# Three pairs of banks for the gate and up products in the ternary feed-forward stages

## The chip, the cores and the metric

The kernel runs on one core of a Trainium2 chip. The metric is the device time of one execution in microseconds; lower is better. A core has five engines that run their own instruction streams and meet by semaphores: TensorE (PE in the rows; PEld are its weight loads), VectorE (DVE), ScalarE (ACT), GpSimd (POOL) and SyncE (SP), which issues DMAs. TensorE writes its products to PSUM, eight banks of 512 fp32 columns by 128 partitions, from which VectorE and ScalarE read them.

## The reference

Two layers on x, 2048 tokens of 256 numbers. Each is half a feed-forward part, attention, and half a feed-forward part again, each on the layer norm of x. The first layer's feed-forward part has ternary weights:

```python
gu = jnp.einsum('bsd,hd->bsh', x, wq_gu)
gate, up = jnp.split(gu, 2, axis=-1)
h = jax.nn.silu(gate) * up
hn = rms_norm(h)
return jnp.einsum('bsh,dh->bsd', hn, wq_p)      # x = x + 0.5 * this
```

h has 1024 columns. rms_norm divides each token's h by the root of its mean square plus eps. The second layer's feed-forward part has no such norm; it keeps the two largest of each four of h.

## The kernel before

It is a row of stages that follow each other with a barrier: set-up of the ternary weights, ffn0a (ternary, 63 to 185 us), attention with its projections, ffn0b (ternary, 723 to 847 us), then the same with the second layer's ffn1a and ffn1b. One function, `ffn_phase` (L299 on), writes all four feed-forward stages; `ternary` is true for the first two. Each engine's order is written out by hand in it.

A stage works through NB = 4 blocks of 512 tokens: block 0 alone, blocks 1 and 2 in a hardware loop, block 3 alone. A block has NCH = 8 chunks of 128 hidden columns. For chunk c of block b, with n = 8b + c:

- TensorE, `gate_up` (L361): 8 matmuls of 512 columns, 4 for gate and 4 for up (two halves of the input width, by high and low part of x). Gate goes to bank `slots[c]`, up to the next. In the ternary stages `slots` is 0, 2, 0, 2, ...: two pairs of banks. It first waits until the multiply of chunk n-2 is done (the semaphore `mul` at n-1).
- ScalarE, `silu` (L431), from the gate bank into one of two buffers. Behind it, for the chunk before: `hi` (L438), the high part of h, and the square (L447). Both wait for the multiply of their chunk, so silu of chunk c+1 is queued behind the multiply of chunk c-1.
- VectorE, `multiply` (L485): h = silu x up bank. Behind it `lo` (L490), the low part of h of the chunk before.
- GpSimd adds the squares of a block up (L590, L593) and takes powers: the inverse of a deviation for layer norm (L136) and of the root mean square (L597).

Between the chunks stand, in TensorE's order: behind chunk 2 `squares` of block b-1 (L383, sums of squares over partitions, into 4 columns of bank 4) and the second half of `down` of block b-1 (L372, 32 matmuls); behind chunk 6 the eight `transposes` of block b+1's normalised x (L143, into banks TB and TB+1, here 4 and 5); behind chunk 7 the first half of `down` of block b, 32 matmuls into banks 6 and 7, which first waits for `residual` of block b-1. In VectorE's order: behind chunk 1 the statistics of block b+1; behind chunk 3 `mean_squares` of block b-1 (L524, reads the 4 columns), then the normalisation of block b+1 (L124, four instructions); behind chunk 6 `residual` of block b-1 (L532, four instructions, reads banks 6 and 7); before chunk 7's multiply the low part of the transposed x (L158), after ScalarE's high part (L151).

In the text "multiply 4" is the multiply of chunk 4 of the block spoken of, and so on.

Of the kernel before, what the change touches and what calls it, by code (L numbers as in the profile page):

```python
# [24 lines left out]
ALU = mybir.AluOpType  # L25
# [3 lines left out]
P = 128  # L29
# [4 lines left out]
NB = TOK // BLK  # L34
TPB = BLK // P
# [3 lines left out]
HID = 4 * D  # L39
NCH = HID // P  # L40
# [13 lines left out]
RMS_EPS = float(np.finfo(np.float32).eps)  # L54
# [7 lines left out]
def named(g, nc, prefix, names):  # L62

    sems = [nc.alloc_semaphore(name=f"{prefix}_{n}") for n in names.split()]
    g.sems += sems
    return namedtuple("Semaphores", names)(*sems)
# [14 lines left out]
def blocks_of(eng, body):  # L81

    body(0)
    with eng.Fori(1, NB - 1) as b:
        body(b)
    body(NB - 1)


def is_first(b):
    return isinstance(b, int) and b == 0  # L90


def is_last(b):
    return isinstance(b, int) and b == NB - 1
# [44 lines left out]
def pe_transpose(e, g, s, b, src, bank=0):  # L139

    for k in range(KD):
        for j in range(TPB):
            ins = e.transpose(g.ps[:, bank + k, j * P:(j + 1) * P], src(j, k), g.ident[:, :])  # L143
    ins.then_inc(s.tr, 1)
# [9 lines left out]
def dve_lo(e, g, s, b, bank=0, half=None):  # L154
    xh, xl = (g.xh, g.xl) if half is None else (g.xh[:, half], g.xl[:, half])
    for k in range(KD):
        e.wait_ge(s.xhi, b * KD + k + 1)
        e.tensor_tensor(xl[:, k, :], g.ps[:, bank + k, :], xh[:, k, :].bitcast(F32), ALU.subtract).then_inc(s.xlo, 1)  # L158
# [140 lines left out]
def ffn_phase(nc, g, name, ternary, out=None, ahead=()):  # L299
# [12 lines left out]
    with ExitStack() as ctx:  # L312
        s = named(g, nc, name, names)

        def sb(n, shape, dt):
            return ctx.enter_context(nc.sbuf_tensor(f"{name}_{n}", shape, dt))
# [6 lines left out]
        if ternary:  # L323
            sq = sb("sq", [P, 2, BLK], F32)
            ssq = sb("ssq", [P, 2, BLK], F32)
            ms, inv = sb("ms", [P, TPB], F32), sb("inv", [P, TPB], F32)
            w_up = [g.wt[:, 0:KD * 2 * HID].rearrange("p (k h) -> p k h", k=KD)]
            w_dn = [g.wt[:, KD * 2 * HID:].rearrange("p (c d) -> p c d", c=NCH)]
            terms = [(0, 0), (0, 1)]
            hs = h32  # L330
            slots, TB = (0, 2, 0, 2, 0, 2, 0, 2), 4
        else:
            ab = sb("abs", [P, 2, GCH, BLK], F32)
            win = sb("win", [P, 6, BLK], BF16)
            rank = sb("rank", [P, GCH, BLK], BF16)
            w_up = [t[:, :].rearrange("p (k h) -> p k h", k=KD) for t in (g.wgu_h, g.wgu_l)]
            w_dn = [t[:, :].rearrange("p (c d) -> p c d", c=NCH) for t in (g.wdn_h, g.wdn_l)]
            terms = [(0, 0), (0, 1), (1, 0)]
            hs = ab
            slots, TB = (0, 2, 4, 0, 2, 4, 0, 4), 2  # L340
        xp, hp = [g.xh, g.xl], [hh, hl]
        block = ctx.enter_context(nc.Block())

# [1 line left out]
        @block.tensor  # L345
        def _(e):
            def gate_up(b, c):
                n = b * NCH + c

                if ternary:  # L350
                    if not (is_first(b) and c < 2):
                        e.wait_ge(s.mul, n - 1)
                elif not (is_first(b) and c < 3) and c != 1:
                    e.wait_ge(s.mul, n - 1 if c in (0, NCH - 1) else n - 2)
                for half in range(2):
                    col = half * HID + c * P
                    for k in range(KD):
                        if c == 0 and half == 0:
                            e.wait_ge(s.xlo, b * KD + k + 1)
                        for q, (w, x) in enumerate(terms):  # L360
                            ins = e.matmul(g.ps[:, slots[c] + half, :], w_up[w][:, k, col:col + P], xp[x][:, k, :],  # L361
                                           start=k == 0 and q == 0, stop=k == KD - 1 and q == len(terms) - 1)
                ins.then_inc(s.gu, 1)

            def down(b, u, tiles=range(TPB)):
                e.wait_ge(s.hlo, b * NCH + u * GCH + GCH)
                if u == 0 and not is_first(b):
                    e.wait_ge(s.res, b)
                for j in tiles:
                    todo = [(i, w, x) for i in range(GCH) for w, x in terms]  # L370
                    for q, (i, w, x) in enumerate(todo):
                        ins = e.matmul(g.ps[:, 6 + j // 2, (j % 2) * D:(j % 2 + 1) * D], hp[x][:, u, i, j * P:(j + 1) * P],  # L372
                                       w_dn[w][:, u * GCH + i, :], start=u == 0 and q == 0 and j % 2 == 0,
                                       stop=u == 1 and q == len(todo) - 1, skip_group_check=True)
                if j == TPB - 1:
                    ins.then_inc(s.dn if u else s.dnh, 1)

            def squares(b):

                e.wait_ge(s.sqc, b * NCH + NCH)  # L380
                for j in range(TPB):
                    for u in range(2):
                        ins = e.matmul(g.ps[:, 4, j:j + 1], ssq[:, u, j * P:(j + 1) * P], g.one_col[:, :],  # L383
                                       start=j == 0 and u == 0, stop=u == 1, skip_group_check=True)
                ins.then_inc(s.sqs, 1)

            def transposes(b):
                e.wait_ge(s.xn, b + 1)
                if not is_first(b):
                    if ternary and not (isinstance(b, int) and b == 1):  # L390
                        e.wait_ge(s.ms, b - 1)
                    if not ternary:
                        e.wait_ge(s.mul, b * NCH - 3)
                pe_transpose(e, g, s, b, lambda j, k: g.xn[:, j, k * P:(k + 1) * P], TB)

            def body(b):
                for c in range(NCH):
                    gate_up(b, c)
                    if ternary:
                        if c == 2 and not is_first(b):  # L400
                            squares(b - 1)
                            down(b - 1, 1)
                        if c == NCH - 1:
                            down(b, 0)
                    elif not is_first(b):
                        if c == 4:
                            down(b - 1, 0)
                        if c == NCH - 2 and not is_last(b):
                            down(b - 1, 1, range(TPB // 2))
                        if c == NCH - 1:  # L410
                            down(b - 1, 1, range(0 if is_last(b) else TPB // 2, TPB))
                    if c == NCH - 2 and not is_last(b):
                        transposes(b + 1)

            transposes(0)
            blocks_of(e, body)
            if ternary:
                squares(NB - 1)
            else:
                down(NB - 1, 0)  # L420
            down(NB - 1, 1)
# [57 lines left out]
        def _(e):  # L479
# [41 lines left out]

            def mean_squares(b):
                e.wait_ge(s.sqs, b + 1)
                e.tensor_scalar(ms[:, :], g.ps[:, 4, 0:TPB], 4.0 / HID, 4.0 * RMS_EPS, ALU.mult, ALU.add).then_inc(s.ms, 1)  # L524

            def residual(b):
                if ternary:
# [8 lines left out]
            def body(b):  # L536
                for c in range(NCH):
                    if c == NCH - 1 and not is_last(b):
                        dve_lo(e, g, s, b + 1, TB)
                    multiply(b, c)  # L540
                    if ternary:
                        if c:
                            lo(b, c - 1)
                        elif not is_first(b):
                            lo(b - 1, NCH - 1)
                        if c == 3 and not is_first(b):
                            mean_squares(b - 1)
                        if c == 6 and not is_first(b):
                            residual(b - 1)
                    elif c >= GCH:  # L550
                        choose(b, 0, c - GCH)
                    elif not is_first(b):
                        choose(b - 1, 1, c)
                    if not is_last(b) and c == 1:
                        dve_stats(e, g, s, b + 1)
                    if not is_last(b) and c == (3 if ternary else 5):
                        dve_normalise(e, g, s, b + 1)
                if not ternary and not is_first(b) and not is_last(b):
                    residual(b - 1)
# [1021 lines left out]
```

## Time and profile before

| | us |
|---|---|
| median of 3 runs | 1806.38 |
| lowest, highest run | 1805.32, 1822.72 |
| the profiled execution: its time | 1802.62 |
| the profiled execution: its span | 1800.4 |

In the rows, a timeline line gives start, duration, engine, line, operation, output<-input, and in brackets how long the engine had been idle and what released it. Recorded ends of matmuls overlap the start of the next one, so the distance between two starts is what one costs.

### The profile page before, as it was taken

Reading aid. Unit: us, or ns where it says so; the run is one execution under the profiler, and the core shown is the slowest. Engines: PE = TensorE matmul, PEld = TensorE weight load, DVE = VectorE, ACT = ScalarE, POOL = GpSimd, SP = SyncE. Lnnn points to the kernel's source line nnn. Section 1 sums busy time; section 2 is a strip of 40 time slices with the busy share of each in tenths; the row PEclk is TensorE's granted clock in tenths of the full one; section 3 lists DMA queues with packets and bytes.
Section 4 is the critical chain, followed back from the end, with each engine's and each line's share of the span. In section 5 each row is a group of like instructions: output and inputs, shape, how many; then the busy total and the mean of one; then the engine's idle time right before and its main releaser. Section 6 shows DMA issues by size and latency. Waiting matters only on the chain. (4 is left out here: it accounts for less than half of the span.)

```text
span 1800.4 us, 33059 instructions
## 1 busy us (share of the span) xinstructions
PE 1556.4 (86%) x13324; PEld 972.3 (54%) x13324; DVE 1283.4 (71%) x1864; ACT 950.9 (53%) x1889; POOL 306.7 (17%) x326
## 2 busy tenths in 40 slices
PE   1598878989999999887799689899999999997996
PEld 0487744444434436676588567444444444366885
DVE  8655647888898832564599786687888988025996
ACT  3345324767777784454334222456686788733342
POOL 5333100000000000232043432000000000030433
PEclk9999869999999999898899888698999999788998
DMA  5000769100000000100100058640000000020000
GB/s 201 24 1 0 127 184 129 34 14 24 13 20 7 2 2 3 46 1 24 35 1 1 1 116 199 87 69 14 20 17 16 11 2 2 2 71 1 12 12 24
DMA packets 37857, 70.54 MB, mean 39 GB/s; under 512 B 5411, under 2 KB 13219, under 8 KB 36645
## 3 DMA queue, kind: packets, MB, share of 16 engines
q1 hardware_dynamic: 37716, 68.58, 16.8%
q8 instruction: 99, 1.62, 0.4%
q14 instruction: 42, 0.34, 0.1%
HBM read 48.90 MB, written 22.15 MB: 39 GB/s over the span
## 5 line engine op out<-in xcount | busy, mean ns | idle before, releaser
L1166 DVE TENSOR_REDUCE l_att_maxima<-psum 128x2 f32<-128x1024 f32 (+3 forms) x640 | 665.0, 1063 | 135.3 <-PE psum L1064 127.6
L1258 ACT ACTIVATE l_att_probs<-psum 128x512 f32<-128x512 f32 (+3 forms) x1280 | 605.6, 531 | 250.3 <-PE psum L1092 227.8
L1109 PE MATMUL psum<-l_att_probs,l_att_v 128*17 128x256 f32 (+2 forms) x4608 | 363.5, 389 | 1.2 <-ACT l_att_o L1265 0.9
L1092 PE MATMUL psum<-l_att_qt,l_kt 51*128 51x512 f32 (+6 forms) x1280 | 331.6, 470 | 7.5 <-ACT l_att_probs L1258 7.5
L1064 PE MATMUL psum<-l_kt,l_att_qt 59*128 59x512 f32 (+7 forms) x1280 | 285.2, 422 | 5.0 <-DVE l_att_maxima L1166 2.6
L1092 PEld LDWEIGHTS psum<-l_att_qt,l_kt 59*128 59x128 f32 (+1 forms) x1280 | 142.6, 194 | 174.0 <-ACT l_att_probs L1258 161.8
L1109 PEld LDWEIGHTS psum<-l_att_probs,l_att_v 128*17 128x17 f32 x4608 | 79.5, 96 | 150.5 <-issue 101.7
L1064 PEld LDWEIGHTS psum<-l_kt,l_att_qt 59*128 59x128 f32 (+1 forms) x1280 | 139.1, 199 | 19.5 <-DVE l_att_maxima L1166 17.4
L1228 POOL CAST l_att_crow<-l_att_cneg 128x16 bf16<-128x16 f32 x32 | 8.1, 252 | 812.6 <-DVE l_att_cneg L1176 812.6
L1061 PE MATMUL psum<-tri 64*128 64x128 bf16 x1024 | 89.1, 237 | 22.0 <-DVE l_att_maxima L1166 18.8
L1090 PEld LDWEIGHTS psum<-tri 64*128 64x128 bf16 x1024 | 33.7, 96 | 101.8 <-ACT l_att_probs L1258 65.6
L1090 PE MATMUL psum<-tri 64*128 64x128 bf16 x1024 | 82.4, 228 | 1.9 <-DMA l_att_qt<-l_att_ct 1.7
L1193 DVE RECIPROCAL l_att_rinv<-psum 128x16 f32<-128x16 f32 x32 | 8.0, 250 | 106.3 <-PE psum L1128 106.3
L1061 PEld LDWEIGHTS psum<-tri 64*128 64x128 bf16 x1024 | 35.8, 101 | 59.8 <-DVE l_att_maxima L1166 34.3
L580 POOL TENSOR_TENSOR ffn1b_hl<-ffn1b_abs,ffn1b_hh 128x512 fp32r<-128x512 f32 x32 | 51.7, 1643 | 84.6 <-ACT ffn1b_hh L438 84.6
L580 POOL TENSOR_TENSOR ffn1a_hl<-ffn1a_abs,ffn1a_hh 128x512 fp32r<-128x512 f32 x32 | 51.7, 1644 | 84.6 <-ACT ffn1a_hh L438 84.6
L136 POOL TENSOR_TENSOR rstd<-var,mhalf 128x4 f32<-128x4 f32 x24 | 24.7, 1027 | 224.8 <-DVE var L115 224.8
L361 PE MATMUL psum<-ffn0b_xh,w_ternary 128*128 128x512 f32 x128 | 53.1, 415 | 9.2 <-DVE ffn0b_h L485 7.8
L361 PE MATMUL psum<-ffn0a_xh,w_ternary 128*128 128x512 f32 x128 | 52.9, 413 | 9.1 <-DVE ffn0a_h L485 7.7
L361 PE MATMUL psum<-ffn1b_xh,wgu_h 128*128 128x512 f32 x128 | 51.5, 402 | 3.9 <-DVE ffn1b_xl L158 2.8
L361 PE MATMUL psum<-ffn1a_xh,wgu_h 128*128 128x512 f32 x128 | 51.3, 400 | 3.9 <-DVE ffn1a_xl L158 2.8
L372 PE MATMUL psum<-wdn_h,ffn1b_hh 128*128 128x256 f32 x128 | 38.8, 303 | 15.6 <-DVE x_resident L532 8.9
(205 smaller groups left out, 2914.5 us busy)
## 6 DMA issues: line engine op xcount, KB each, us to landing
l_kt<-qk_scratch SPq DMA_DIRECT2D x48, 256.0 KB, 10.6
qk_scratch<-l_att_kv_parts SPq DMA_DIRECT2D x22, 512.0 KB, 7.3
l_att_qt<-qk_scratch SPq DMA_DIRECT2D x168, 64.0 KB
qk_scratch<-y SPq DMA_DIRECT2D x10, 512.0 KB, 10.7
set_raw<-in_w_gu SPq DMA_DIRECT2D x2, 1024.0 KB, 6.4
x_resident<-in_x SPq DMA_DIRECT2D x1, 2048.0 KB, 15.4
y<-in_w_gu SPq DMA_DIRECT2D x1, 2048.0 KB, 8.1
raw_down<-in_w_dn SPq DMA_DIRECT2D x2, 1024.0 KB, 8.0
```

The lines of the kernel that those rows point to most:

```text
L136: e.tensor_tensor(g.rstd[:, :], g.var[:, :], g.mhalf[:, :], ALU.pow).then_inc(s.rstd, 1)
L361: ins = e.matmul(g.ps[:, slots[c] + half, :], w_up[w][:, k, col:col + P], xp[x][:, k, :], start=k == 0 and q == 0, stop=k == KD - 1 and q ...
L372: ins = e.matmul(g.ps[:, 6 + j // 2, (j % 2) * D:(j % 2 + 1) * D], hp[x][:, u, i, j * P:(j + 1) * P], w_dn[w][:, u * GCH + i, :], start=u ...
L580: e.tensor_tensor(hl[:, c // GCH, c % GCH, :], hs[:, c // GCH, c % GCH, :], hh[:, c // GCH, c % GCH, :].bitcast(F32), ALU.subtract).then_i ...
L1061: e.matmul(g.ps[:, bank + x, w - P:w], g.tri[half, (2 + m) * P:(3 + m) * P], g.tri[half, m * P:(m + 1) * P], start=m == 0, stop=False, ski ...
L1064: e.matmul(g.ps[:, bank + x, 0:w], qt[rows_of(x), pair, t * P:(t + 1) * P], g.kt[rows_of(x), pair, c * BLK:c * BLK + w], start=c < qb, sto ...
L1090: e.matmul(g.ps[:, i % SB, off:off + P], g.tri[rows, c * P:(c + 1) * P], g.tri[rows, (2 + c) * P:(3 + c) * P], start=c == 0, stop=False, s ...
L1092: e.matmul(g.ps[:, i % SB, off:BLK], g.kt[rows_of(x), hp, kt * P:(kt + 1) * P], qt[rows_of(x), hp, off:BLK], start=u >= TPB, stop=True, sk ...
L1109: ins = e.matmul(g.ps[h * VW:h * VW + HD + 1, OB, lo:hi], g.v[:, kt, STEPS[st][1] * HG + h, :], pr[:, un % PB, h, lo:hi], start=u == 0 and ...
L1166: e.tensor_reduce(mp[:, st % 2, 2 * p:2 * p + 2, t, c], g.ps[:, bank:bank + 2, 0:w], AX.X, ALU.max).then_inc(s.mx, 1)
L1228: e.tensor_copy(cr[:, 0], whole).then_inc(s.cp, 1)
L1258: e.activation(pr[:, un % PB, h, off:BLK], g.ps[:, i % SB, off:BLK], ACT.Exp, scale=HD ** -0.5).then_inc(s.ex, 1)
```

## The change

In the ternary stages too, gate and up now go through three pairs of banks in the order 0, 2, 4, 0, 2, 4, 0, 4, and the transposes through banks 2 and 3 (TB = 2). `gate_up` waits for the multiply that read its pair last: of chunk n-3, for chunks 0 and 7 of chunk n-2; chunk 1 waits for none. The transposes wait for multiply 4 of the block in which they stand, in place of `mean_squares`. `squares` goes to bank TB and waits for multiply 1 of its block, the last reader of that bank. `mean_squares` moves on VectorE from behind chunk 3 to behind chunk 2, and chunk 4, the next to write that bank, waits for it. The stages of the second layer keep their order.

```diff
-            slots, TB = (0, 2, 0, 2, 0, 2, 0, 2), 4
         else:
...
-            slots, TB = (0, 2, 4, 0, 2, 4, 0, 4), 2
+        slots, TB = (0, 2, 4, 0, 2, 4, 0, 4), 2
...
-                if ternary:
-                    if not (is_first(b) and c < 2):
-                        e.wait_ge(s.mul, n - 1)
-                elif not (is_first(b) and c < 3) and c != 1:
+                if not (is_first(b) and c < 3) and c != 1:
                     e.wait_ge(s.mul, n - 1 if c in (0, NCH - 1) else n - 2)
+                if ternary and c == 4 and not is_first(b):
+                    e.wait_ge(s.ms, b)
...
-            def squares(b):
+            def squares(b, last):
 
                 e.wait_ge(s.sqc, b * NCH + NCH)
+                e.wait_ge(s.mul, last)
                 for j in range(TPB):
                     for u in range(2):
-                        ins = e.matmul(g.ps[:, 4, j:j + 1], ssq[:, u, j * P:(j + 1) * P], g.one_col[:, :],
+                        ins = e.matmul(g.ps[:, TB, j:j + 1], ssq[:, u, j * P:(j + 1) * P], g.one_col[:, :],
...
                 if not is_first(b):
-                    if ternary and not (isinstance(b, int) and b == 1):
-                        e.wait_ge(s.ms, b - 1)
-                    if not ternary:
-                        e.wait_ge(s.mul, b * NCH - 3)
+                    e.wait_ge(s.mul, b * NCH - 3)
...
-                            squares(b - 1)
+                            squares(b - 1, b * NCH + 2)
...
-                squares(NB - 1)
+                squares(NB - 1, NB * NCH - 3)
...
-                e.tensor_scalar(ms[:, :], g.ps[:, 4, 0:TPB], 4.0 / HID, 4.0 * RMS_EPS, ALU.mult, ALU.add).then_inc(s.ms, 1)
+                e.tensor_scalar(ms[:, :], g.ps[:, TB, 0:TPB], 4.0 / HID, 4.0 * RMS_EPS, ALU.mult, ALU.add).then_inc(s.ms, 1)
...
-                        if c == 3 and not is_first(b):
+                        if c == 2 and not is_first(b):
                             mean_squares(b - 1)
```

## Rows read from the trace of the kernel before

**Rows 1.** The first line of the page.
```profile
span 1800.4 us, 33059 instructions
```

**Rows 2.** Windows view: length, busy PE, PEld, DVE, ACT, POOL, clock, DMA share, GB/s.
```profile
63.00:184.00 121.00, 108.50 (x608) 93.68 (x608) 68.64 (x131) 58.36 (x105) 40.29 (x31) 0.97 0.00 1
723.00:846.00 123.00, 109.21 (x608) 94.20 (x608) 69.14 (x134) 58.36 (x105) 40.28 (x31) 0.93 0.02 10
```

**Rows 3.** Waits view of PE in ffn0a: us in total, times, longest.
```profile
PE psum L361 <- DVE ffn0a_h L485: 7.7, 4, 2.3
```

**Rows 4.** Timeline, block 0: PE and DVE in ffn0a, PE in ffn0b.
```profile
77.12 0.50 PE L361 MATMUL psum<-ffn0a_xh,w_ternary 128*128 128x512 f32 x1 [0.94 <-DVE ffn0a_h L485]
...
82.54 0.67 DVE L485 TENSOR_TENSOR ffn0a_h<-ffn0a_silu,psum 128x512 f32<-128x512 f32 x1
...
83.74 0.68 DVE L485 TENSOR_TENSOR ffn0a_h<-ffn0a_silu,psum 128x512 f32<-128x512 f32 x1
...
83.27 0.50 PE L361 MATMUL psum<-ffn0a_xh,w_ternary 128*128 128x512 f32 x1 [2.19 <-DVE ffn0a_h L485]
...
85.22 1.03 PE L143 MATMUL psum<-consts,ffn0a_xn 128*128 128x128 f32 x8
86.01 0.47 PE L361 MATMUL psum<-ffn0a_xh,w_ternary 128*128 128x512 f32 x1
...
87.94 0.28 PE L372 MATMUL psum<-w_ternary,ffn0a_hh 128*128 128x256 f32 x1
...
742.97 0.50 PE L361 MATMUL psum<-ffn0b_xh,w_ternary 128*128 128x512 f32 x1 [2.23 <-DVE ffn0b_h L485]
...
749.23 0.28 PE L372 MATMUL psum<-w_ternary,ffn0b_hh 128*128 128x256 f32 x1
```

**Rows 5.** Timeline of PE, blocks 1 and 2: chunk 6 and the down matmuls.
```profile
110.90 0.50 PE L361 MATMUL psum<-ffn0a_xh,w_ternary 128*128 128x512 f32 x1 [2.28 <-DVE ffn0a_h L485]
...
117.38 0.36 PE L372 MATMUL psum<-w_ternary,ffn0a_hh 128*128 128x256 f32 x1
...
140.39 0.50 PE L361 MATMUL psum<-ffn0a_xh,w_ternary 128*128 128x512 f32 x1 [2.30 <-DVE ffn0a_h L485]
...
146.27 0.36 PE L372 MATMUL psum<-w_ternary,ffn0a_hh 128*128 128x256 f32 x1 [1.05 <-DVE x_resident L532]
...
801.05 0.50 PE L361 MATMUL psum<-ffn0b_xh,w_ternary 128*128 128x512 f32 x1 [2.30 <-DVE ffn0b_h L485]
...
808.13 0.35 PE L372 MATMUL psum<-w_ternary,ffn0b_hh 128*128 128x256 f32 x1 [0.64 <-DVE x_resident L532]
```

**Rows 6.** Timeline of DVE, block 1 of ffn0a.
```profile
106.97 3.27 DVE L124 TENSOR_SCALAR ffn0a_xn<-x_resident,mv,rstd 128x256 f32 x4
110.17 0.68 DVE L485 TENSOR_TENSOR ffn0a_h<-ffn0a_silu,psum 128x512 f32<-128x512 f32 x1
...
114.38 0.69 DVE L485 TENSOR_TENSOR ffn0a_h<-ffn0a_silu,psum 128x512 f32<-128x512 f32 x1 [1.73 <-ACT ffn0a_silu L431]
...
115.58 1.65 DVE L532 SCALAR_TENSOR_TENSOR x_resident<-psum,ffn0a_inv,x_resident 128x256 f32 x4
```

**Rows 7.** Timeline, block 1: mean squares on DVE, then ACT.
```profile
106.90 0.15 DVE L524 TENSOR_SCALAR ffn0a_ms<-psum 128x4 f32<-128x4 f32 x1
...
111.41 0.62 ACT L447 ACTIVATE ffn0a_sq<-ffn0a_h 128x512 f32<-128x512 f32 x1
113.66 0.60 ACT L431 ACTIVATE ffn0a_silu<-psum 128x512 f32<-128x512 f32 x1 [1.63 <-PE psum L361]
```

**Rows 8.** Timeline, block 1: multiply 1 on DVE, squares on PE.
```profile
96.34 0.69 DVE L485 TENSOR_TENSOR ffn0a_h<-ffn0a_silu,psum 128x512 f32<-128x512 f32 x1 [0.42 <-ACT ffn0a_silu L431]
...
97.32 1.84 PE L383 MATMUL psum<-one_col,ffn0a_ssq 128*128 128x1 f32 x16
```

**Rows 9.** Windows view, columns as in rows 2.
```profile
112.00:116.00 4.00, 4.00 (x16) 3.44 (x15) 2.27 (x6) 1.67 (x4) 0.56 (x1) 0.57 0.02 4
...
180.00:300.00 120.00, 94.77 (x770) 67.09 (x769) 71.05 (x138) 42.03 (x86) 9.50 (x22) 0.80 0.80 149
```

## The prediction

> **What bounds the kernel now.** The profiled execution spans 1800.4 us [rows 1]; its own time is 1802.62 us. The change touches only the two ternary feed-forward stages, ffn0a and ffn0b, so I read the windows view of these first: together 244 us, TensorE busy 108.50 of 121 and 109.21 of 123 us, VectorE only 68.6 and 69.1 [rows 2]. TensorE sets the pace there, and what can be won is its idle time. The waits view of TensorE names it: 7.7 us in ffn0a before gate and up matmuls (L361), in four waits, released by the multiply of L485 [rows 3]. I looked these up in the timeline: in block 0 at chunk 4 (0.94) and at chunk 6 (2.19), and at chunk 6 in blocks 1 and 2 (2.28, 2.30); ffn0b repeats the pattern [rows 4, 5]. Block 3 has none, since it normalises no next block.
>
> The cause stands in VectorE's timeline. After multiply 3 it normalises the next block (L124, x4), which takes 3.27 us; multiply 4 can only come then, ending at 110.85 [rows 6]. Chunk 6 waits with the condition "multiply n-2 done", which with two pairs of banks means chunk 4, and starts at 110.90 [rows 5]. The 3.27 us stay: nothing in the change touches what VectorE, ScalarE or GpSimd compute. So the full 15 us of both stages can't be won. What must be found is which wait ends last once chunk 6 no longer waits.
>
> **The change, part by part.**
>
> *Three pairs of banks.* Chunk 4 now needs only multiply 1, chunk 5 multiply 2, and chunk 6 multiply 3. The four waits of each stage go. The transposes take over the wait for multiply 4, and chunk 7 still waits for multiply 5, as it did.
>
> *Block 0.* Chunk 4 starts about 0.94 us earlier, so chunks 4 and 5 end near 81.08 - 0.94 = 80.1 (81.08 is 83.27 - 2.19), and chunk 6, 1.95 us long (83.27 to 85.22, where chunk 6 ran before the transposes), is over near 82.1. Multiply 4 ends at 82.54 + 0.67 = 83.21 and lets the transposes go; they take 0.8 us (85.22 to 86.01). Multiply 5 ends at 83.74 + 0.68 = 84.42 [rows 4]. So chunk 7 starts at 84.47 (0.05 us from a release to the matmul, as 83.27 against 83.21), not at 86.01, and the down matmuls 1.93 us later (86.01 to 87.94), at 86.40. They have no residual to wait for. Gain 87.94 - 86.40 = **1.54 us**. From multiply 4's end to the down matmuls this is 86.40 - 83.21 = 3.19 us. In ffn0b multiply 4 ends at 742.97 - 0.05 = 742.92, so they start at 746.11 against 749.23 [rows 4]: **3.12 us**. It is twice as much since there the clock fell during chunk 6: 6.26 us from chunk 6 to the down matmuls against 4.67 in ffn0a, thus 1.59 us for one fall.
>
> *Blocks 1 and 2.* Here the down matmuls (L372) also wait for residual (L532), which VectorE runs after multiply 6. I follow that chain in block 1 of ffn0a [rows 6, 7]. Mean squares (0.15 us, but 0.07 from its start to the next one's) is gone from before the normalisation, so multiply 4 ends at 110.78. ScalarE then makes the high part and the square of chunk 4, which end 1.18 us after multiply 4 did (112.03 - 110.85): 111.96. Chunk 6 left TensorE at about 108.62 + 1.9 = 110.5, so silu 6, which started at 113.66 because it waited for TensorE, starts at about 111.9 and ends at 112.5. Multiply 6 follows 0.12 us later (114.26 to 114.38), at 112.62; residual starts 1.20 us after it (114.38 to 115.58), at 113.82, lasts 1.65 and ends at 115.47; the down matmuls start 0.15 us behind it (115.58 + 1.65 = 117.23, against 117.38), at 115.62. That is 4.84 us after multiply 4. Chunk 7, from 112.0 (multiply 5 ends 1.21 us after multiply 4, as in block 0: 84.42 - 83.21) to about 114.1, is over before: **residual ends last**, and TensorE is left with about 1.5 us of idle time in front of the down matmuls where block 2 had 1.05. Applied to the rows: ffn0a block 1 gains 117.38 - 115.62 = **1.76**; block 2: 140.34 - 0.07 + 4.84 = 145.11 against 146.27, **1.16**; ffn0b block 1 has the same 5.88 us from chunk 6 to down as this one, **1.16**; ffn0b block 2: 801.00 - 0.07 + 4.84 = 805.77 against 808.13, **2.36** [rows 5]. The larger two again hold a fall of the clock: 6.48 and 7.08 us from chunk 6 to down, against 5.88, thus 0.60 and 1.20 each.
>
> *Block 3.* All its chunks follow each other already, and its residual wait stays: 0.
>
> *Squares in bank TB.* The 16 recorded matmuls are the same. New is the wait for multiply 1, behind which the second half of down (b-1), chunk 3 and all later chunks queue. Multiply 1 ends at 97.03, squares starts at 97.32 [rows 8], so 0.29 us of cover: chunk 2's own matmuls, 1.8 us long. The other blocks look the same. Cost 0. If the cover were gone by x, every middle and last block would lose x, six times in all; I see nothing that moves multiply 1.
>
> *Mean squares at chunk 2.* It waits for squares, over at 97.32 + 1.84 = 99.16 [rows 8]. VectorE gets to it behind multiply 2 and low part 1, and these follow silu 2 of a chunk that left TensorE at 97.4: 97.4 + 0.2 + 0.6 (silu) + 0.1 + 0.6 + 0.6 = 99.5 at the earliest, so it doesn't stall. Nor is silu 3 near, which needs chunk 3 behind 32 down matmuls. It costs 0 there and takes 0.07 off the later place (counted). The new wait of chunk 4 comes near 108.62 - 3.8 = 104.8 (two chunks of 1.9 us before chunk 6's wait), over 4 us after mean squares: 0. GpSimd takes the inverse in the same place, behind its additions. No DMA is issued or moved, and SP's queue isn't passed.
>
> *Sum.* ffn0a 1.54 + 1.76 + 1.16 = 4.46; ffn0b 3.12 + 1.16 + 2.36 = 6.64; together 11.1 us. 1802.62 - 11.1 = 1791.5, a ratio of 0.9938. The profiled execution lies 0.2% under the median of the runs, so on the median of 1806.38 this is **1795.3 us**.
>
> **The clock.** The sum takes TensorE at 2.4 GHz in all six places. Before, three of the six waits of 2.19 to 2.33 us were followed by a stretch at 1.2 GHz (a mean of 0.57 over 112 to 116 in ffn0a [rows 9]), three not. After the change the idle time in front of the transposes is 83.27 - 82.1 = 1.2 us in block 0 and 0.3 us in the middle ones, then 0.3 in front of chunk 7, then 1.5 in front of down. Each piece is shorter than any that a fall followed at chunk 6. One in front of down of 1.86 us in block 3 was also followed by a fall.
>
> The Trainium skill, TensorE: Matmul & The Clock Gate (Part 4: PE-mode transpose), says that full clock doesn't engage for transposes, as they don't count as busy in the same way. By that rule the pause of block 0 is 84.47 - 82.1 = 2.4 us, longer than each pause before, and the sum would be 7.9 us; no row here parts it from the other reading.
>
> **Rivals.** (a) *Transposes don't hold the clock.* Then block 0 pauses for 2.4 us in both stages and pays 1.59 us twice; in blocks 1 and 2 it is 1.6 us and holds. 11.1 - 3.2 = 7.9: 1798.5. For it: waits of 2.2 us were followed by falls three times in six; against: three times not. 0.15. (b) *The clock falls three times, as before,* since the pauses keep a similar total. Then each stage keeps its share: 2 x (1.54 + 1.16 + 1.16) = 7.7: 1798.7. 0.15. (c) *The middle blocks give nothing,* as residual doesn't move with multiply 4 (GpSimd's inverse or down of the block before would hold it). Only 1.54 + 3.12 = 4.7 us come: 1801.7. Against it: VectorE stands idle before multiply 6 for ScalarE, and that for TensorE. 0.08. (d) *Slower: the clock falls on both sides of chunk 7.* The one pause becomes three, and the middle blocks get a longer one before down. With eight falls in the four middle blocks and two in block 0, at 1.59 each, 15.9 us are lost against 11.1: 1811.2. It decides from seven falls on. 0.04. (e) *The gain meets a different clock later.* Over 180 to 300 us the mean clock is 0.80 [rows 9], so 48 us at the lower level; starting that stretch 5 us earlier may change how many there are, by up to 24 us in either direction, at half of that, 12, with the sum: 1783 or 1807. 0.13, most of it small.
>
> **How the numbers follow.** The forecast has 0.45 and, with rivals (a) to (c), 0.83. The bounds: no fall and a little help later gives 1789; rival (c) at 1801.7 with one fall more gives 1803. Range 1789 to 1803. About 1% is what can be told from no change. 1% is 18 us; only (e) reaches it, or a run spread like that of before (1805.32 to 1822.72). Faster by over 1%: 0.08; within: 0.89; slower: 0.03.
>
> **What would show it.** Right: the L485 release of TensorE's L361 wait is down to a few tenths at chunk 7, and waits for L485 or L124 appear before the transposes (L143), about 1.2 us in block 0 and 0.3 in blocks 1 and 2; the wait of L372 for L532 rises by about 0.5 in block 2 and is near 1.5 in block 1; ffn0a is 4.5 us shorter, ffn0b 6.6; silu 6 waits for no TensorE; squares wait for nothing; the mean clock of ffn0b rises above 0.93. Wrong: idle time before squares, residual where it was against multiply 4, or more stretches at the lower clock than before.

## The result and the profile after

| | before | after |
|---|---|---|
| median | 1804.76 us (20 runs) | 1797.4 us (20 runs) |
| lowest, highest | 1788.81, 1827.86 | 1774.12, 1815.73 |
| ratio after / before | | 0.9942, 95% interval 0.9914 to 0.997 |
| profiled execution: span, mean clock | 1800.4 us, 0.930 | 1795.6 us, 0.927 |
| ffn0a, first transposes to end of last residual | 122.38 us | 117.29 us |
| ffn0b, the same | 123.76 us | 119.71 us |

The kernel is 0.4% (medians) to 0.6% (ratio) faster, in the place forecast. The ratio leaves out the runs that lie more than 1.5% above the fastest of their kernel; the medians count all 20. Line numbers after are lower by 1 to 4: L359 is L361 of before, L370 the down matmuls (L372), L382 squares (L383), L481 the multiply (L485), L520 mean squares (L524), L528 the residual (L532).

First the waits view of TensorE over the first stage of the kernel after (us in total, times, longest). It answers [rows 3]:

```profile
PE psum L370 <- DVE x_resident L528: 4.7, 3, 1.9
PE psum L143 <- DVE ffn0a_h L481: 2.9, 3, 1.8
```

No gate and up matmul (L359) waits for a multiply any more. In place of these 7.7 us TensorE has new waits of 2.9 us in front of the transposes, and its waits for the residual rose from 2.9 us (1.05 and 1.86) to 4.7. The timeline of TensorE after, in block 0 and then in block 1, answers [rows 4, 5]:

```profile
82.67 1.07 PE L143 MATMUL psum<-consts,ffn0a_xn 128*128 128x128 f32 x8 [1.77 <-DVE ffn0a_h L481]
83.78 0.50 PE L359 MATMUL psum<-ffn0a_xh,w_ternary 128*128 128x512 f32 x1
...
85.73 0.28 PE L370 MATMUL psum<-w_ternary,ffn0a_hh 128*128 128x256 f32 x1
...
108.70 1.10 PE L143 MATMUL psum<-consts,ffn0a_xn 128*128 128x128 f32 x8 [0.54 <-DVE ffn0a_h L481]
109.90 0.50 PE L359 MATMUL psum<-ffn0a_xh,w_ternary 128*128 128x512 f32 x1
...
113.44 0.36 PE L370 MATMUL psum<-w_ternary,ffn0a_hh 128*128 128x256 f32 x1 [1.43 <-DVE x_resident L528]
```

Chunk 6 is over before the transposes wait; what had been one pause of 2.28 us is now 0.54 before them and 1.43 before down. VectorE's timeline in block 1 shows why, against [rows 6, 7]:

```profile
98.64 0.15 DVE L520 TENSOR_SCALAR ffn0a_ms<-psum 128x4 f32<-128x4 f32 x1
103.47 0.69 DVE L481 TENSOR_TENSOR ffn0a_h<-ffn0a_silu,psum 128x512 f32<-128x512 f32 x1 [4.68 <-ACT ffn0a_silu L427]
...
104.68 3.37 DVE L124 TENSOR_SCALAR ffn0a_xn<-x_resident,mv,rstd 128x256 f32 x4
107.97 0.67 DVE L481 TENSOR_TENSOR ffn0a_h<-ffn0a_silu,psum 128x512 f32<-128x512 f32 x1
...
111.64 1.65 DVE L528 SCALAR_TENSOR_TENSOR x_resident<-psum,ffn0a_inv,x_resident 128x256 f32 x4
```

Mean squares now stands where VectorE has 4.68 us with nothing to do. The normalisation still takes its 3.4 us between multiply 3 and multiply 4. Multiply 4 ends at 108.64, and the down matmuls start 4.80 us later.

**The spread of the whole time is mostly clock.** In 74 runs of the kernel before, in four sessions, the time in us follows 3156 - 1455 x (mean granted clock) with a scatter of 2.0 us, for means from 0.913 to 0.942. The line is fitted, and says nothing of clocks outside that range. A clock lower by 0.01 costs 14.5 us, more than the change gains. So I give for each kernel also its distance to this line, "at the same clock". The changed kernel's 40 runs lie 7.9 us under it, with a standard error of 0.3 (one run more, 1931.74 us at a mean clock of 0.732, is left out; the line would give 2091 there and doesn't reach that far). The line doesn't count what a kernel wins by a higher clock. The stage lengths of a profile, and the waits in it, are sharper than either, and the verdicts below go by them.

### The profile page after: what moved, and what is told of

It is laid out like the page before. It is cut to its first block and busy times, and to the rows that moved or that the text cites. A ratio compares the mean times of both kernels' runs of the same rounds, so it can differ in the third digit from the quotient of the medians.

```text
span 1795.6 us, 33067 instructions
## 1 busy us (share of the span) xinstructions
PE 1559.2 (87%) x13324; PEld 976.5 (54%) x13324; DVE 1287.0 (72%) x1864; ACT 950.0 (53%) x1889; POOL 305.4 (17%) x326
## 5 line engine op out<-in xcount | busy, mean ns | idle before, releaser
L1060 PEld LDWEIGHTS psum<-l_kt,l_att_qt 59*128 59x128 f32 (+1 forms) x1280 | 139.3, 200 | 19.3 <-DVE l_att_maxima L1162 18.3
L359 PE MATMUL psum<-ffn1a_xh,wgu_h 128*128 128x512 f32 x128 | 51.7, 404 | 3.9 <-DVE ffn1a_xl L158 2.8
L359 PE MATMUL psum<-ffn1b_xh,wgu_h 128*128 128x512 f32 x128 | 51.5, 402 | 3.9 <-DVE ffn1b_xl L158 2.8
L359 PE MATMUL psum<-ffn0b_xh,w_ternary 128*128 128x512 f32 x128 | 52.5, 410 | 1.7 <-DVE ffn0b_xl L158 1.4
L370 PE MATMUL psum<-wdn_h,ffn1a_hh 128*128 128x256 f32 x128 | 39.5, 309 | 15.4 <-DVE x_resident L528 8.9
L359 PE MATMUL psum<-ffn0a_xh,w_ternary 128*128 128x512 f32 x128 | 51.4, 401 | 1.7 <-DVE ffn0a_xl L158 1.4
## 6 DMA issues: line engine op xcount, KB each, us to landing
qk_scratch<-y SPq DMA_DIRECT2D x10, 512.0 KB, 10.3
```

Of the source, the lines that this page charges most:

```text
L1060: e.matmul(g.ps[:, bank + x, 0:w], qt[rows_of(x), pair, t * P:(t + 1) * P], g.kt[rows_of(x), pair, c * BLK:c * BLK + w], start=c < qb, sto ...
```

## The experiments

**late_ms: mean squares put back.** The rest of the change stays.

```diff
-                        if c == 2 and not is_first(b):
+                        if c == 3 and not is_first(b):
                             mean_squares(b - 1)
```

> One part undone: mean squares goes back behind chunk 3 on VectorE, the three pairs of banks stay. Theory: chunk 4, which writes that bank, then waits about 2.3 us for it (it could start 1.9 us after chunk 3, mean squares would be done about 4.2 us after it), each middle block loses 1.0 us at its down matmuls and the last block 2.3 us, 4.2 us a stage, so 8.4 us in all: most of the gain goes. Rival (the place of mean squares is free, 0.15 us of work either way): the same stage lengths as the changed kernel, 117.3 and about 120.

The waits view of TensorE over ffn0a:

```profile
PE psum L359 <- DVE ffn0a_ms L520: 6.7, 3, 2.3
PE psum L370 <- DVE x_resident L528: 4.0, 3, 1.9
PE psum L143 <- DVE ffn0a_h L481: 1.8, 1, 1.8
```

Three waits of 2.26, 2.26 and 2.17 us at chunk 4, as expected. The stages took 124.98 and 124.84 us, longer than before the change: beside the waits, the clock fell behind two of the three in each stage. They are 12.8 us longer together than in the kernel after, where 8.4 was expected without these falls. At the same clock this kernel is 4.4 us slower than the one before (10 runs; ratio 1.0013, 0.9961 to 1.0065). The three pairs pay only together with the move, since mean squares shares a bank with chunk 4.

**two_pairs_norm_early: VectorE's burst moved, no third pair.** An edit to the kernel before:

```diff
-                    if not is_last(b) and c == (3 if ternary else 5):
+                    if not is_last(b) and c == ((3 if is_first(b) else 2) if ternary else 5):
                         dve_normalise(e, g, s, b + 1)
```

> The kernel before with its two pairs of banks, but the normalisation of the next block moved from behind chunk 3 to behind chunk 2 on VectorE in blocks 1 and 2 (block 0 unchanged), where VectorE stands idle for over 4 us. Theory (the cause of the waits is the burst on VectorE between multiply 3 and multiply 4, the third pair only lets TensorE run over it): the waits of 2.3 us at chunk 6 of blocks 1 and 2 vanish without any third pair, the down matmuls of these blocks start 2.5 us earlier each than in the kernel before at full clock, 5 us a stage, and block 0 keeps its 0.94 and 2.2 us: ffn0a near 117 us. Rival (two pairs are too few for the pace of TensorE whatever VectorE does): the waits stay near 2 us and the stage near 122.

The waits view over ffn0a:

```profile
PE psum L372 <- DVE x_resident L532: 4.0, 3, 1.9
PE psum L361 <- DVE ffn0a_h L485: 3.2, 2, 2.2
```

The two waits left at L361 are those of block 0. The stages took 117.64 and 116.96 us, and the runs lie 10.3 us under the line (10 runs; ratio 0.9946, 0.9905 to 0.9988): as good as the change, with two pairs of banks. The rival fell: in blocks 1 and 2 two pairs are enough for TensorE's pace.

**norm_early: the same move on top of the change.**

> The changed kernel with the normalisation of the next block behind chunk 2 on VectorE in blocks 1 and 2, ahead of the burst. Theory: multiply 4 no longer comes late, the pause of 0.54 us before the transposes goes, and the residual moves up with silu 6: down matmuls 1.3 us earlier in each of the two blocks, 2.6 us a stage, ffn0a near 114.7. Rival (the normalisation has no part in what ends last, which is the residual alone): down matmuls where they are against chunk 3, 117.3.

Stages 113.78 and 114.19 us, near the 114.7 expected, and 13.5 us under the line (9 runs; ratio 0.9929, 0.9889 to 0.9969). From the second half of down to the next block's first half, in blocks 1 and 2, TensorE needs 16.64 us in the kernel after (96.80 to 113.44) and 15.13 here; with two pairs and the move it was 15.17. So once the burst is gone, the third pair is worth nothing in the middle blocks, and what it still gives is block 0: from multiply 4 to down 3.2 us in place of 4.73 (two pairs, ffn0b), 1.5 us a stage, and more where the clock falls.

**res_early: residual behind chunk 2,** and GpSimd's inverse ahead of its additions.

```diff
-                        if c == 6 and not is_first(b):
+                        if c == 2 and not is_first(b):
                             residual(b - 1)
...
+                    if not is_first(b):
+                        inverse(b - 1)
                     sum_squares(b, 0)
-                    if not is_first(b):
-                        inverse(b - 1)
                     sum_squares(b, 1)
```

> The changed kernel with residual of the block before moved from behind chunk 6 to behind chunk 2 on VectorE (and GpSimd's inverse moved ahead of the additions, so that it is ready), the normalisation left behind chunk 3. Theory (residual ends last before the down matmuls): the waits of 1.43, 1.43 and 1.86 us in front of down vanish, and the clock fall behind the last of them with it (1.5 us): 6.2 us a stage, ffn0a near 111. Rival (something else, chunk 3's high and low parts or multiply 5, holds the down matmuls or chunk 7 as long): under 2 us a stage.

The waits view over ffn0a:

```profile
PE psum L143 <- DVE ffn0a_h L481: 2.9, 3, 1.8
PE psum L359 <- DVE ffn0a_xl L158: 1.4, 1, 1.4
PE psum L382 <- POOL ffn0a_ssq L589: 1.2, 1, 1.2
```

All three waits for the residual are gone: it did end last. The stages took 114.24 and 113.94 us, 13.8 us under the line (4 runs; ratio 0.9891, 0.9838 to 0.9945). The expected 111 was missed by a new wait: in the last block squares now wait 1.23 us for GpSimd's sum, which the residual's wait had covered. In ffn0a the clock fell behind it; in ffn0b it fell behind the pause before the transposes of block 0 instead.

**both_early and both_early_again: both moves,** with GpSimd's inverse ahead of its additions as in res_early.

> Both moves together, behind chunk 2: normalisation, then residual. Theory: TensorE has no pause from chunk 3 to the end of the first half of down in blocks 1 to 3; saved against the changed kernel 0.54 + 1.43 in blocks 1 and 2, 1.86 and a clock fall of 1.5 in block 3: 7.3 us a stage, ffn0a near 110, 14.6 us in all and 25 against the kernel before (ratio near 0.986). Rival (VectorE is now late for multiply 3, since the two moves fill its idle 4.7 us: 1.4 to 3.3 plus 1.65): a new pause at chunk 6, gain under 8 us.

> Normalisation and residual behind chunk 2, the kernel that had the shortest stages, once more and with more rounds, since its first ratio rests on few runs. Theory: the two stages are 10.2 to 10.6 us shorter each than in the kernel before, some 20 us in all, a ratio of 0.989; at the same mean clock 19 us less, as in the first six runs. Rival (the 20 us of the first time were luck with the clock): a ratio of 0.993, as the changed kernel has.

The waits view over ffn0a, then VectorE's timeline in block 1:

```profile
PE psum L143 <- DVE ffn0a_h L481: 1.7, 1, 1.7
PE psum L359 <- DVE ffn0a_xl L158: 1.4, 1, 1.4
PE psum L382 <- POOL ffn0a_ssq L590: 1.2, 1, 1.2
```

```profile
101.81 0.15 DVE L520 TENSOR_SCALAR ffn0a_ms<-psum 128x4 f32<-128x4 f32 x1
101.88 1.37 DVE L124 TENSOR_SCALAR ffn0a_xn<-x_resident,mv,rstd 128x256 f32 x4
104.29 1.66 DVE L528 SCALAR_TENSOR_TENSOR x_resident<-psum,ffn0a_inv,x_resident 128x256 f32 x4 [1.04 <-PE psum L370]
...
106.64 0.69 DVE L481 TENSOR_TENSOR ffn0a_h<-ffn0a_silu,psum 128x512 f32<-128x512 f32 x1 [0.69 <-ACT ffn0a_silu L427]
```

No pause is left in blocks 1 and 2, and both pieces fit into VectorE's idle time: it still waits 0.69 us for silu 3. So the rival, a new pause at chunk 6, didn't come, but the expected 110 was missed in the last block: squares wait 1.23 us as in res_early, with a clock fall behind it in all four stages. Stages 112.16 and 113.20 us, then 113.53 and 112.14 in the second profile. Ratio 0.9818 (0.9751 to 0.9886), then 0.9826 (0.9765 to 0.9888), and 19.3 us under the line over 12 runs. The stages are 20.8 and 20.5 us shorter than before, which by itself is a ratio of 0.989. The medians of all runs give the same, 0.989 and 0.988; that the two ratios above are lower is not explained by the stages, and they rest on six runs each. This version beats both kernels.

**all_spread: block 0's normalisation too.** One instruction behind chunk 3, one behind chunk 4, two behind chunk 5, on top of both moves.

> The kernel with both moves (normalisation and residual behind chunk 2 in blocks 1 and 2), and in block 0 the normalisation of block 1 spread: one instruction behind chunk 3, one behind chunk 4, two behind chunk 5. Theory: the pause of 1.77 us before the transposes of block 0 shrinks to under 0.5, stage 1.3 to 1.8 us shorter than with both moves alone (112.2 us with one clock fall), so near 110.6, and the fall behind that pause, seen in 3 of 14 cases, goes. What stays is the last block's wait for GpSimd's sum, 1.23 us. Rival: the pause only moves to chunk 7, since multiply 5 comes late: 112.

The transposes of block 0 in TensorE's timeline:

```profile
84.49 0.93 PE L145 MATMUL psum<-consts,ffn0a_xn 128*128 128x128 f32 x4 [3.00 <-DVE ffn0a_xn L125]
```

The theory failed, and the rival too: 114.33 and 114.74 us, longer than without it. Multiply 4 came 2 to 3 us sooner, but the transposes need the last normalised tile, which was now queued behind multiply 5 and ended at 84.43 (VectorE's timeline):

```profile
83.71 0.72 DVE L125 TENSOR_SCALAR ffn0a_xn<-x_resident,mv,rstd 128x256 f32<-128x256 f32 x2
```

The pause grew from 1.77 to 3.00 us, with a clock fall behind it in both stages. Ratio 0.9927 (0.989 to 0.9963), 17.7 us under the line (12 runs) against 19.3. In block 0 all of the normalisation is due before the transposes, so spreading it past chunk 4 only makes it late.

**squares_late: the new wait of squares made longer.**

```diff
-                            squares(b - 1, b * NCH + 2)
+                            squares(b - 1, b * NCH + 3)
```

> The changed kernel with the new wait of squares made longer: it waits for multiply 2 in place of multiply 1, 3.1 us later. Theory (TensorE sets the pace there, nothing later in the block gives slack): each of the three blocks with squares loses the full 3.1 us, 9.4 us a stage and 18.8 in all, and up to 1.6 us more where a clock fall follows. Rival (the pauses of 0.5 and 1.4 us later in blocks 1 and 2 take part of it up): some 5 us a stage in place of 9.4.

The waits view over ffn0a, and the windows view of the 7 us behind the first of these pauses (columns as in rows 2):

```profile
PE psum L382 <- DVE ffn0a_h L481: 7.5, 3, 3.0
```

```profile
100.00:107.00 7.00, 7.00 (x35) 7.00 (x35) 0.28 (x2) 0.00 (x0) 1.27 (x1) 0.52 0.00 0
```

Nothing took the waits up: the pauses of 0.54 and 1.43 us behind them stayed. In block 3, which has no statistics on VectorE, the wait was 1.50 us and not 3.1, so the waits came to 7.5 us a stage in place of 9.4. But the stages took 134.44 and 134.40 us, 17.2 and 14.7 us more than after. Nearly all of the rest is clock: behind each pause of 3 us TensorE ran for 6.8 us at 1.2 GHz (a mean of 0.52 above), and behind the one of 1.50 us for 3.4. Half speed for 6.8 us loses 3.4 us, twice my price for a fall, 1.59. The ratio was 1.0175 (1.0075 to 1.0276; 4 runs).

**transposes_x8: what holds the clock.** The eight transposes are issued eight times over.

> The changed kernel, in which the eight transposes of blocks 1 and 2's place (those written for blocks 2 and 3, and for block 1 behind block 0) are issued eight times over, 64 in place of 8, some 6 us of nothing but transposes on TensorE. If transposes do not hold the clock (rival (a)), it falls to 1.2 GHz inside each of the six stretches and the transposes slow from 0.10 to about 0.2 us each; if they hold it like matmuls, the clock stays at 2.4 GHz and a stretch takes 64 x 0.1 = 6.4 us.

The windows view, over two such stretches of ffn0a and one of ffn0b (the first PE column is busy time, the third from the end the clock):

```profile
83.82:90.75 6.93, 6.93 (x64) 6.93 (x65) 2.85 (x5) 2.56 (x5) 1.29 (x1) 1.00 0.01 2
115.70:122.60 6.90, 6.90 (x64) 6.90 (x65) 4.54 (x9) 2.60 (x5) 1.36 (x1) 1.00 0.01 2
760.00:766.90 6.90, 6.90 (x63) 6.90 (x64) 2.85 (x5) 2.56 (x5) 1.29 (x1) 1.00 0.00 1
```

The clock stayed at 2.4 GHz through 64 transposes in all six stretches, even right behind a pause of 1.72 us. Rival (a) is out: these fp32 transposes hold the clock like matmuls (one profile). The rule cited for it from the Trainium skill, TensorE: Matmul & The Clock Gate (Part 4: PE-mode transpose), doesn't hold for them here; the measurement decides. The trace lists them as MATMUL and doesn't show whether they ran in the mode that the rule is about.

**after_again and after_third: the changed kernel twice more.**

> The changed kernel once more, for the places where the clock falls. If the pauses before the transposes of block 0 (1.78 us in both stages) are what decides, as under rival (a), both block 0s fall to the lower clock again or both hold; if it depends on how the pause lies against the clock's own rhythm, one may fall and the other not, and not the same as in the first profile (there ffn0b fell, ffn0a did not). In blocks 1 and 2 no fall is expected by the forecast, four or more by rival (d). Stage lengths from the first transposes to the end of the last residual: about 117.3 us for ffn0a and 118 to 121 for ffn0b. Multiply 4 to the down matmuls in the middle blocks 4.8 us.

> The changed kernel beside it on the same chip: stage lengths of 116 to 118 us (ffn0a) and 117 to 120 (ffn0b); a ratio to the kernel before of 0.993 by the stages alone; what it lies off that is clock outside the two stages.

ffn0a took 115.90 and 116.74 us, ffn0b 116.96 and 117.11; the first profile of the two was below what had been expected (about 117.3, and 118 to 121), since the clock fell nowhere in its stages once TensorE was at full speed. The pauses were the same to 0.04 us in all six stages seen; the lengths differ by clock falls and by how soon TensorE reached full speed at the start. The ratios, 0.999 (0.9944 to 1.0035) and 0.992 (0.9877 to 0.9963), show how little such a ratio tells of a change this small: in one session the change isn't clear of noise. The medians of all runs are steadier: 0.9959, 0.9954 and 0.9946 in the three sessions.

**Where the clock fell,** over all profiles of this study, by the granted clock of short windows:

| pause of TensorE | places | falls behind it |
|---|---|---|
| 0.54, then chunk 7, then 1.43 (blocks 1, 2; the changed kernel, three profiles) | 12 | 0 |
| 0.9 to 1.1, at chunk 4 in block 0 or in front of down (blocks 1, 2) | 18 | 0 |
| 1.23, then squares (block 3, residual early, four profiles) | 8 | 7 |
| 1.50, then squares (block 3, squares_late) | 2 | 2 |
| 1.7 to 1.8, then transposes (block 0, three pairs, ten profiles) | 20 | 3 |
| 1.86 in front of down in block 3 | 18 | 12 |
| 2.2 to 2.3 at chunk 4 or 6 | 14 | 8 |
| 3.0 | 6 | 6 |

The length of a pause alone doesn't decide: 1.23 us in front of squares (16 matmuls of one column) drew more falls than 1.77 us in front of transposes.

## Why the prediction was right, and where it was off

**The cause and the next limit: right.** The four waits a stage went, the transposes took over the one for multiply 4, and the residual came to end last, as res_early showed by moving it. From multiply 4 to the down matmuls I had worked out 3.19 us in block 0 and 4.84 in the middle ones; ffn0a after shows 85.73 - 82.52 = 3.21 and 113.44 - 108.64 = 4.80. The wait before down in block 2 was to be near 1.5 and was 1.43.

**Edits costed at nothing: right.** Squares waited for nothing in the kernel after, and squares_late shows what the 0.29 us of cover stand before. Mean squares behind chunk 2 stalled nobody; late_ms shows that leaving it would have cost more than the whole gain. I had counted 0.07 us for it, and not said that the move is what makes the third pair pay.

**Pauses: one mis-sized.** Before the transposes of block 0 I expected 1.2 us and it was 1.77 (0.3 and 0.54 in the middle blocks). About half of that is that I had added recorded ends of matmuls where starts should have been counted, since ends overlap the next start. The rest is that chunk 4 took 1.98 us behind its wait before and 1.81 without one, and that the transposes start 0.14 us behind multiply 4, where I had taken 0.05. It changed nothing in the sum, which went by VectorE's times.

**The sum, by its terms.** It was 4.46 for ffn0a and 6.64 for ffn0b, 11.1 in all. The profile shows 5.09 and 4.05, 9.1 in all. ffn0a got 0.69 us more in block 0, since TensorE was at full speed that much sooner at the start: chunk 1 took 1.84 us, and 2.45 before (the records of the clock begin only at 69.7 and 71.2 us). ffn0b got 2.1 us less there: at its start TensorE was at the lower clock for longer, 0.94 us (multiply 4 came 20.43 us after the first transposes, against 19.49), and the clock fell in chunk 7, 1.15 us, and 0.40 more in down. Its block 2 gained 2.3 us against 2.36 forecast. So the step that fell short is "the sum takes TensorE at 2.4 GHz in all six places": it was so in five of six, and in the two further profiles in six of six. The windows view of this fall:

```profile
742.00:746.00 4.00, 4.00 (x16) 3.37 (x15) 1.80 (x4) 2.13 (x5) 1.28 (x1) 0.57 0.01 2
```

I had also said that ffn0b's mean clock would rise above 0.93. Over the stage it was 0.935 against 0.932, hardly a sign.

**From the stages to the whole.** The span fell by 4.8 us, not by the 9.1 of the stages. The other stages took 4.3 us more, with the same work; the mean clock over the span was 0.927 against 0.930. That is rival (e), small, in this one profile. Over 40 runs, at the same clock, the gain is 7.9 us, which is just the forecast without any clock fall saved: 2 x (1.54 + 1.16 + 1.16) = 7.7. The medians of 20 runs differ by 7.4. The 3.4 us that I had added for falls avoided are real in the stages (no fall in 12 places of blocks 1 and 2, where the profile before had two in four), but the noise of the clock elsewhere is several times that. The 1795.3 forecast was on a median of 1806.38 of three runs, and against the 1797.4 measured it is 2.1 us low. That nearness is partly luck: the median before was 1.6 us lower over 20 runs than over the three, so the gain of the medians, 7.4 us, is two thirds of the 11.1 forecast.

**The rivals.** (a) is refuted by transposes_x8. (b), as many falls as before, is not what three profiles show: one fall in 18 blocks (0 to 2 of six stages), against three in six before. The time alone would not have told: (a) and (b) stood at 1798.5 and 1798.7, nearer to the 1797.4 than the forecast. (c) is refuted: from the second half of down to the next first half the middle blocks take 16.6 us each, against 17.7 to 19.0 before. (d) never began: 0 of 12. Its price was too low, though, for a change that makes pauses of 3 us: squares_late shows 6.8 us of low clock behind each.

## What to carry to other kernels

When an engine waits for a buffer, look first for the burst of another engine that frees it late, and for the idle time in which that burst would cost nothing: moving four normalising instructions by one chunk did with two pairs of banks what the third pair did. A second consumer of a shared bank (here four columns of sums) has to be read early, or a new pair brings a new wait. Judge a gain of half a per cent by stage lengths and waits over several profiles, or at the same mean clock, since the ratio moved between 0.992 and 0.999 for the same kernel.

## What the runs showed of the hardware that I had not expected

- The whole time follows the mean granted clock at 14.5 us per 0.01, and the same kernel ranges over 0.916 to 0.944, 1774 to 1816 us.
- A pause of 3.0 us was followed by 6.8 us at 1.2 GHz (3.4 in one place of six), one of 2.2 us by 3.4 us or by none. Pauses of 1.86 us in front of down drew a fall in 12 of 18 places, those of 1.77 us in front of transposes in 3 of 20, and those of 1.23 us in front of squares in 7 of 8; what parts them is open.
- The four normalising instructions take 3.27 us behind chunk 3 [rows 6], 2.27 behind chunk 2 in norm_early, and 1.37 behind chunk 2 in both_early. The difference is GpSimd. Behind chunk 3 of the kernel after it ran nearly all the while that they did (104.68 to 108.05):

```profile
104.47 1.45 POOL L589 TENSOR_TENSOR ffn0a_ssq<-ffn0a_ssq,ffn0a_sq 128x512 f32<-128x512 f32 x1 [4.60 <-ACT ffn0a_sq L443]
106.28 1.29 POOL L589 TENSOR_TENSOR ffn0a_ssq<-ffn0a_ssq,ffn0a_sq 128x512 f32<-128x512 f32 x1 [0.36 <-ACT ffn0a_sq L443]
107.53 1.07 POOL L593 TENSOR_TENSOR ffn0a_inv<-ffn0a_ms,mhalf 128x4 f32<-128x4 f32 x1
```

In norm_early one addition ran beside the first of them:

```profile
99.58 1.38 POOL L586 TENSOR_TENSOR ffn0a_ssq<-ffn0a_sq 128x512 f32<-128x512 f32 x1
99.81 2.27 DVE L124 TENSOR_SCALAR ffn0a_xn<-x_resident,mv,rstd 128x256 f32 x4
```

In both_early only the small inverse (128x4) did, for most of their time (101.88 to 103.25):

```profile
102.04 1.25 POOL L594 TENSOR_TENSOR ffn0a_inv<-ffn0a_ms,mhalf 128x4 f32<-128x4 f32 x1 [0.36 <-DVE ffn0a_ms L520]
```

One by one it is plain. In the two stages of all 13 profiles, 118 normalising instructions for a next block began while an addition of GpSimd was running. Each took 1.29 to 1.41 us and ended 0.15 to 0.16 us behind that addition's end. The other 194 took 0.40 us each, among them 60 that began while the inverse was running. So VectorE stands still here until the addition is over, and that stretches 1.37 us of normalisation to 3.27. As an estimate from these durations, 1.9 of the 2.3 us that chunk 6 waited before come from it; no run tests that by itself. The Trainium skill, SBUF — State Buffer (Who interferes with whom), says that VectorE's copy-like and scalar instructions can take the port pair that it shares with GpSimd, and that whoever comes first holds it for a whole instruction while the other is blocked. The trace agrees for the additions. For the inverse, which lasts 1.01 to 1.25 us and blocked none, it shows no such block. That the port is the cause is not shown.
